# Attention on one core: the values' matmuls between a step's two score pairs, both maxima behind the second

## The chip, the cores and the metric

The kernel runs on one core of a Trainium2 chip. The metric is the device time of one execution in microseconds. An engine's work is named as in the profile: PE is TensorE (PEld its weight loads), DVE VectorE, ACT ScalarE, POOL GpSimd, SP SyncE.

## The reference

Four blocks act on x (4 batches of 512 tokens, 512 wide): a quantised gated linear layer, a mixture of experts, cross attention with rotary positions, and a second mixture of experts. The change lies in the attention:

```python
q = (x @ Wq).reshape(b, n, N_HEADS, HEAD_DIM)       # 32 heads of 16
k, v = jnp.split(ctx @ Wkv, 2, axis=-1)
q = apply_axial_rope(q, pos_map)
k = apply_axial_rope(k, ctx_pos_map)
logits = jnp.einsum('bqhd,bkhd->bhqk', q, k) * scale
w = jax.nn.softmax(logits, axis=-1)
attn = jnp.einsum('bhqk,bkhd->bqhd', w, v)
return attn.reshape(b, n, N_HEADS * HEAD_DIM) @ Wout + bout
```

## The kernel before

`attention` (L1657) works on units of eight heads of one batch: (b, c) with c from 0 to 3, sixteen units in all. Every engine runs the same list of turns (`turns`, L1791): four turns for a batch -1 that only prepare, four for batch 0, a hardware loop over batches 1 and 2 (`Fori`), four for batch 3, and two that finish. A turn (b, c) has eight steps. In each step of TensorE's turn:

- `scores` (L1974) makes transposed scores of one head for 128 keys and 512 queries, in PSUM banks 4 and 5 in turn; four of them a step (h = 0 to 3), S0 to S3 below. Each waits until ScalarE's exponential of two scores before (`exp_done`) has left its bank. ScalarE's `exps` (L2083) writes E, E0 to E3 below.
- `maxima` (L1988) makes scores of a later unit the other way round, two heads at once for 128 queries, in banks 0 and 1 (pair 0) or 2 and 3 (pair 1). VectorE reduces each pair to row maxima (`a_top`, L2223), 16 reductions a turn, number n = 2 * step + pair. The next `maxima` into the same banks waits for that reduction (`maxed`). After reduction 7 `cut_max` (L2184 to L2192) splits the maxima into three bfloat16 parts; slot 10 turns them, ScalarE copies them, and GpSimd writes them to memory and back into the rows of Q (L1901, L1910), for the scores of the next unit.
- `values` (L2006) multiplies V by the exponentials of the step before, into bank 6: four heads in four column strips, float32. After the fourth and the eighth step ScalarE copies bank 6 (`take_sum`, L2092).
- `slot(n)` (L1959) runs the side jobs of `jobs(b, c, n)` (L1765). All use bank 7. Before a job TensorE waits until the one before it has been consumed (`DONE`, L1953). The kinds: "x" turns the normalised tokens (L1924, consumed by ScalarE), "q" projects queries (L1929, ScalarE), "o" turns the values' result (L1940, VectorE normalises it, L2202 and L2208), "a" turns the attention output (L1945, ScalarE), "m" turns the maxima (L1934, ScalarE), "p" is the output projection of 128 tokens (L1950; VectorE adds it into X, L2214).

Every turn has q in slot 0, o in slots 4 and 11, a in 8, m in 10. A turn with c == 0 has besides p in slots 12, 14 and 15 and x in 13 and 15 (behind p); one with c == 1 has two x ahead of q in slot 0 and p in slot 2. The c == 0 turn of batch 3 has no x.

VectorE's turn goes through n = 0 to 15: reduction n, then the tasks of n, then the consumption of a job of slot n:

```python
for fn in tasks[n]:
    fn()
outs(n)
```

The tasks of every turn are the pair swap of q behind reduction 2 (L2173) and `cut_max` behind 7. At c == 0 come the next batch's statistics behind 0 to 3, their aggregation behind 4 (ScalarE takes the root at the start of step 3, L2097, with two loads of its function table), the normalisation behind 8 (L2155) and the bias behind 12 (L2161).

Of the kernel before, what the change touches and what calls it, by code (L numbers as in the profile page):

```python
# [1425 lines left out]
class SideJobs:  # L1426
# [55 lines left out]
    def count(self, b, kind, n):  # L1482

        return b * len(self.JOBS) + self.JOBS.index((kind, n)) + 1
# [172 lines left out]
def attention(nc, X, PS, identf, identb, ones_b, tg, ln_eps, tgate, Wq, Wout, bout, tables_dram, k_parts, v_dram, routed):  # L1657
# [22 lines left out]
    with ExitStack() as s:  # L1680
# [69 lines left out]
        def is_unit(b, c):  # L1750
            return not isinstance(b, int) or 0 <= 4 * b + c < NU
# [4 lines left out]
        def before(b, c, n):  # L1756

            c -= n
            while c < 0:
                b, c = b - 1, c + DC  # L1760
            while c >= DC:
                b, c = b + 1, c - DC
            return b, c
# [40 lines left out]
        def n_unit(unit, per=1):  # L1804

            b, c = unit
            return b * (DC * per) + (c + 1) * per

        def n_ring(unit, per):

            return (unit[0] + 1) * per
# [9 lines left out]
        def n_st(unit, step, h):  # L1821
            b, c = unit
            return b * (DC * 32) + c * 32 + step * 4 + h + 1
# [12 lines left out]
        def is_first(unit, n=1):  # L1836

            return isinstance(unit[0], int) and 4 * unit[0] + unit[1] - n < 0
# [75 lines left out]
        @block.tensor  # L1914
        def _(pe):
            pe.wait_ge(w_loaded, 48)
            B = PS[:, 7, :]

            def do(kind, unit, extra):
                b, c = unit  # L1920
                if kind == "x":
                    pe.wait_ge(xh_ready, b + 1)
                    for t in range(TB):
                        last = nc.tensor.transpose(B[:, t * P:(t + 1) * P], xh[:, t, extra * P:(extra + 1) * P], identf[:])  # L1924
                    last.then_inc(x_turned, 1)
                if kind == "q":
                    pe.wait_ge(xT_ready, (b + 1) * DC)
                    for d in range(DC):
                        last = nc.tensor.matmul(B, wq[:, d, c * P:(c + 1) * P], xT[:, d, :], start=(d == 0), stop=(d == DC - 1))  # L1929
                    last.then_inc(q_turned, 1)  # L1930
                if kind == "m":
                    pe.wait_ge(mcut_ready, n_unit(unit))
                    for t in range(TB):
                        last = nc.tensor.transpose(PS[0:3 * HU, 7, t * 64:(t + 1) * 64].bitcast(BF16),  # L1934
                                                   mcut[:, t].rearrange("p i h -> p (i h)"), identb[:])
                    last.then_inc(m_turned, 1)
                if kind == "o":
                    pe.wait_ge(OT_ready, n_unit(unit, 2) - 1 + extra)
                    for t in range(TB):
                        last = nc.tensor.transpose(B[:, t * P:(t + 1) * P], OT[:, t * P:(t + 1) * P], identf[:])  # L1940
                    last.then_inc(o_turned, 1)
                if kind == "a":
                    pe.wait_ge(o_normed, n_unit(unit, 2))
                    for t in range(TB):
                        last = nc.tensor.transpose(B[:, t * P:(t + 1) * P], attn[:, t, c * P:(c + 1) * P], identf[:])  # L1945
                    last.then_inc(a_turned, 1)
                if kind == "p":
                    pe.wait_ge(aT_ready, (b + 1) * DC)
                    for d in range(DC):
                        last = nc.tensor.matmul(B, attnT[:, d, extra * P:(extra + 1) * P], wo[:, d, :], start=(d == 0), stop=(d == DC - 1))  # L1950
                    last.then_inc(projected, 1)

            DONE = {"x": (xT_ready, lambda u, e: u[0] * DC + e + 1), "q": (qf_ready, lambda u, e: n_unit(u)),  # L1953
                    "m": (mT_ready, lambda u, e: n_unit(u)), "o": (o_normed, lambda u, e: n_unit(u, 2) - 1 + e),
                    "a": (aT_ready, lambda u, e: n_unit(u)), "p": (x_added, lambda u, e: u[0] * TB + e + 1)}
            prior = [None]

            def turn(b, c):
                def slot(n):  # L1959
                    for job in jobs(b, c, n):  # L1960
                        if prior[0] is not None:

                            sem_, count = DONE[prior[0][0]]
                            pe.wait_ge(sem_, count(prior[0][1], prior[0][2]))
                        do(*job)
                        prior[0] = job

                if not isinstance(b, int) and c == 0:

                    prior[0] = [j for n in range(16) for j in jobs(*before(b, c, 1), n)][-1]  # L1970
                if isinstance(b, int) and b == NB - 1 and c == 0:
                    prior[0] = [j for n in range(16) for j in jobs(b - 1, DC - 1, n)][-1]

                def scores(unit, step, h):  # L1974
                    if not is_unit(*unit):
                        return
                    k, head, kt = unit[1], (step // 4) * 4 + h, step % 4
                    if step == 0 and h == 0:
                        pe.wait_ge(m_loaded, n_unit(unit, 32))
                        if is_first(unit):  # L1980
                            pe.wait_ge(ones_ready, 4 * RING)
                    if not (is_first(unit) and step == 0 and h < 2):
                        pe.wait_ge(exp_done, n_st(unit, step, h) - 2)
                    o, rows_ = head % 2, (MAX_AT[0] + 3, P)[head % 2]
                    nc.tensor.matmul(PS[:, 4 + h % 2, :], K6[k][0:rows_, o, head // 2, kt * P:(kt + 1) * P], Q6[k][0:rows_, o, head // 2, :],  # L1985
                                     start=True, stop=True).then_inc(st_done, 1)

                def maxima(unit, h, pair):  # L1988
                    if not is_unit(*unit):
                        return  # L1990
                    k = unit[1]
                    if h == 0 and pair == 0:
                        pe.wait_ge(kv_loaded[k], n_ring(unit, 16 * (2 * SLOTS + 1)))
                        pe.wait_ge(q_loaded[k], n_ring(unit, 16 * 2 * SLOTS))
                        if is_first(unit):
                            pe.wait_ge(ones_ready, 4 * RING)
                    if not (is_first(unit) and h == 0):
                        pe.wait_ge(maxed, n_max(unit, h, pair) - 2)
                    t = 2 * (h % 2) + pair
                    for o in range(2):  # L2000
                        at = slice(o * FOUR, (o + 1) * FOUR)
                        last = nc.tensor.matmul(PS[:, 2 * pair + o, :], Q6[k][at, o, h // 2, t * P:(t + 1) * P], K6[k][at, o, h // 2, :],  # L2002
                                                start=True, stop=True)
                    last.then_inc(scored, 1)

                def values(unit, step):  # L2006
                    if not is_unit(*unit):
                        return
                    k, kt = unit[1], step % 4
                    pe.wait_ge(exp_done, n_st(unit, step, 3))  # L2010
                    if kt == 0 and not (is_first(unit) and step == 0):

                        pe.wait_ge(OT_ready, n_unit(unit, 2) - 2 + step // 4)
                    for h in range(4):
                        last = nc.tensor.matmul(PS[32 * h:32 * h + 32, 6, :], V[k][:, kt, (step // 4) * 4 + h, :], E[step % 2][:, h, :],  # L2015
                                                start=(kt == 0), stop=(kt == 3))
                    last.then_inc(pv_done, 1)

                heads = max_heads(b, c)
                for step in range(8):  # L2020
                    scores((b, c), step, 0)
                    scores((b, c), step, 1)
                    maxima(*heads[step], 0)
                    slot(2 * step)
                    scores((b, c), step, 2)
                    scores((b, c), step, 3)
                    maxima(*heads[step], 1)
                    if step == 0:
                        values(before(b, c, 1), 7)
                    else:  # L2030
                        values((b, c), step - 1)
                    slot(2 * step + 1)

            turns(pe, turn)
# [574 lines left out]
```

## Time and profile before

| | |
|---|---|
| median of 3 runs | 1495.58 us (1495.02 to 1496.68) |
| the profiled execution | 1494.6 us, its span 1493.1 us |
| TensorE busy | 1186.9 us |
| VectorE busy | 847.4 us |
| ScalarE busy | 649.5 us |
| GpSimd busy | 401.5 us |
| mean granted clock of TensorE | 0.902 of full speed |

The attention's first score starts at 794.29 us of the span and its last values' matmuls at 1322.48 us. A profile's time is that of one execution; the span runs from its first to its last instruction. Busy times of matmuls overlap with those of weight loads, and the ends of matmuls are modelled.

### The profile page before, as it was taken

What the parts mean: (1) busy time and instruction counts of PE and PEld (TensorE: products, weight loads), DVE (VectorE), ACT (ScalarE), POOL (GpSimd) and SP (SyncE); (2) the same over time, 40 slices, a digit from 0 to 9 for tenths busy, and PEclk for the clock granted to TensorE, in tenths of its full rate; (3) what the DMA queues carried; (4) which work ended last, traced back from release to release, by engine and by line L of the source; (5) the groups of instructions that cost most, each with busy time, mean ns of one, the idle gap of its engine ahead of it and who ended that gap; (6) DMA issues with size and microseconds to landing.
All of it is one profiled execution on the core that took longest, in us unless ns stands there. A gap on an engine that the chain in (4) does not pass through costs nothing. (4 is left out here: it accounts for less than half of the span.)

```text
span 1493.1 us, 18209 instructions
## 1 busy us (share of the span) xinstructions
PE 1186.9 (79%) x5251; PEld 517.3 (35%) x5317; DVE 847.4 (57%) x1314; ACT 649.5 (44%) x1145; POOL 401.5 (27%) x474
## 2 busy tenths in 40 slices
PE   2657566679988999993337899899899999875897
PEld 2333334345544444441101222332232223222453
DVE  3585857641344555521468787667757776415534
ACT  1333232345532222226304666556746665733543
POOL 0505051411113222212453332222303320005332
PEclk8777787889998999997657999999999999996999
DMA  5141311244324444426163332222312330007011
GB/s 197 43 140 34 126 69 57 95 162 136 113 96 170 157 143 147 139 92 200 57 186 104 98 108 75 78 69 81 92 47 84 94 90 7 3 1 85 29 43 43
DMA packets 106348, 141.46 MB, mean 95 GB/s; under 512 B 20788, under 2 KB 75572, under 8 KB 106280
## 3 DMA queue, kind: packets, MB, share of 16 engines
q1 hardware_dynamic: 87912, 111.77, 23.1%
q0 software_dynamic: 18368, 28.85, 7.4%
q8 instruction: 35, 0.57, 0.2%
q14 instruction: 33, 0.27, 0.1%
HBM read 97.44 MB, written 46.27 MB: 96 GB/s over the span
## 5 line engine op out<-in xcount | busy, mean ns | idle before, releaser
L2223 DVE TENSOR_REDUCE a_top<-PS 128x2 f32<-128x1024 f32 x256 | 309.3, 1223 | 114.7 <-PE PS L2002 107.6
L2083 ACT ACTIVATE a_E<-PS 128x512 f32<-128x512 f32 x512 | 277.7, 597 | 134.7 <-PE PS L1985 134.6
L1985 PE MATMUL PS<-a_Q,a_K 99*128 99x512 bf16 (+1 forms) x467 | 161.3, 391 | 33.2 <-ACT a_E L2083 20.5
L1251 PE MATMUL PS<-f_W,f_GT 128*128 x312 | 142.2, 599 | 0.0
L2002 PE MATMUL PS<-a_K,a_Q 64*128 64x512 bf16 x512 | 105.0, 408 | 43.6 <-issue 19.3
L2015 PE MATMUL PS<-a_E,a_V 128*32 128x512 f32 x1024 | 138.0, 612 | 0.4 <-ACT a_E L2083 0.4
L1985 PEld LDWEIGHTS PS<-a_Q,a_K 99*128 99x128 bf16 (+1 forms) x512 | 41.5, 97 | 188.7 <-ACT a_E L2083 165.7
L1307 DVE TENSOR_TENSOR f_H<-f_SG,PS 128x256 f32<-128x256 f32 x39 | 16.4, 422 | 125.8 <-ACT f_SG L1291 125.8
L1251 PEld LDWEIGHTS PS<-f_W,f_GT 128*128 128x128 f32 x312 | 57.2, 193 | 57.5 <-issue 57.5
L1641 POOL TENSOR_TENSOR a_qf<-a_qf,a_tab 128x512 f32<-128x512 f32 x16 | 20.6, 1290 | 206.6 <-DVE a_swapped L2173 206.6
L1270 PE MATMUL PS<-f_W,f_HT 128*128 x156 | 73.3, 593 | 0.0
L2002 PEld LDWEIGHTS PS<-a_K,a_Q 64*128 64x128 bf16 x512 | 24.7, 94 | 130.0 <-issue 79.8
L1929 PE MATMUL PS<-a_xT,a_wq 128*128 128x512 f32 x128 | 64.4, 650 | 3.7 <-ACT a_xT L2056 3.0
L1291 ACT ACTIVATE f_SG<-PS 128x256 f32<-128x256 f32 x39 | 14.9, 383 | 110.7 <-PE PS L1251 110.7
L2544 PE MATMUL PS<-f_W,f_xb 128*128 128x512 bf16 x249 | 61.9, 391 | 0.5 <-issue 0.2
L1950 PE MATMUL PS<-a_wo,a_attnT 128*128 128x512 f32 x128 | 59.2, 605 | 3.7 <-DVE X L2214 2.6
L837 PE MATMUL PS<-f_W,f0r_xT 128*128 128x512 f32 x128 | 58.3, 598 | 0.0
L1351 POOL DMA_INDIRECT a_rows<-f_y,l_pos x32 | 36.3, 1135 | 68.3 <-POOLq L54 40.6
L2334 POOL TENSOR_TENSOR f_H<-f_HF,f_gates 128x512 bf16<-128x512 f32 x32 | 33.4, 1044 | 73.5 <-DVE f_HF L2415 73.5
L1297 ACT COPY f_Y<-PS 128x512 f32<-128x512 f32 x39 | 22.8, 585 | 60.5 <-PE PS L1270 60.5
L1217 POOL DMA_INDIRECT f_G<-f_xn,f_idx x39 | 41.0, 1050 | 29.4 <-POOL f_idx L1214 28.7
L2415 DVE TENSOR_TENSOR f_HF<-f_SG,PS 128x512 f32<-128x512 f32 x32 | 22.0, 688 | 46.5 <-ACT f_SG L2473 46.5
(351 smaller groups left out, 1982.1 us busy)
## 6 DMA issues: line engine op xcount, KB each, us to landing
f0r_raw<-in_L_ffn_W_dram SPq DMA_DIRECT2D x24, 512.0 KB, 5.3
a_K<-k_parts SPq DMA_DIRECT2D x192, 64.0 KB, 2.2
a_Q<-a_q_parts SPq DMA_DIRECT2D x192, 64.0 KB, 2.2
f_y<-f_Y SPq DMA_DIRECT2D x39, 256.0 KB, 2.0
v_units<-V SPq DMA_DIRECT2D x16, 512.0 KB, 3.7
a_V<-v_units SPq DMA_DIRECT2D x16, 512.0 KB, 3.5
k_parts<-f_k_parts SPq DMA_DIRECT2D x16, 384.0 KB, 3.4
a_q_parts<-a_parts SPq DMA_DIRECT2D x16, 384.0 KB, 2.6
```

The lines of the kernel that those rows point to most:

```text
L837: last = nc.tensor.matmul(PS[:, 5, 0:2 * I], xT[b % 2][:, c, t * P:(t + 1) * P], W13[:, E, c, :], start=(c == 0), stop=(c == DC - 1))
L1217: pool.indirect_dma_start(out=G[k][:], out_offset=None, in_=xn_dram, in_offset=bass.IndirectOffsetOnAxis(ap=idx[:, k:k + 1].bitcast(U32), ...
L1251: last = nc.tensor.matmul(PS[:, 2 + k % 2, 0:2 * I], GT[k][:, c, :], W13[:, bass.ds(e, 1), c, :].rearrange("p a n -> p (a n)"), start=(c = ...
L1270: last = nc.tensor.matmul(PS[:, 6 + k % 2, :], HT[k][:, c, :], W2[:, bass.ds(e, 1), c, :].rearrange("p a n -> p (a n)"), start=(c == 0), s ...
L1929: last = nc.tensor.matmul(B, wq[:, d, c * P:(c + 1) * P], xT[:, d, :], start=(d == 0), stop=(d == DC - 1))
L1950: last = nc.tensor.matmul(B, attnT[:, d, extra * P:(extra + 1) * P], wo[:, d, :], start=(d == 0), stop=(d == DC - 1))
L1985: nc.tensor.matmul(PS[:, 4 + h % 2, :], K6[k][0:rows_, o, head // 2, kt * P:(kt + 1) * P], Q6[k][0:rows_, o, head // 2, :], start=True, st ...
L2002: last = nc.tensor.matmul(PS[:, 2 * pair + o, :], Q6[k][at, o, h // 2, t * P:(t + 1) * P], K6[k][at, o, h // 2, :], start=True, stop=True)
L2015: last = nc.tensor.matmul(PS[32 * h:32 * h + 32, 6, :], V[k][:, kt, (step // 4) * 4 + h, :], E[step % 2][:, h, :], start=(kt == 0), stop=( ...
L2083: nc.scalar.activation(E[step % 2][:, h, :], PS[:, 4 + h % 2, :], ACT.Exp).then_inc(exp_done, 1)
L2223: nc.vector.tensor_reduce(top[:, h - h % 2:h - h % 2 + 2, t], PS[:, 2 * pair:2 * pair + 2, :], AX.X, ALU.max).then_inc(maxed, 1)
L2544: last = nc.tensor.matmul(PS[:, 2 * h + m, :], xb[b % 2][:, c, t * P:(t + 1) * P], W13[:, c, m, h * HE:(h + 1) * HE, :].rearrange("p e i - ...
```

## The change

In each step the values move from behind the second maxima to between the score pairs, behind the even slot; the first maxima move to behind the second score pair, so that both stand there together. The odd slot stays last. ScalarE's, VectorE's, GpSimd's and SyncE's programs are as before.

```diff
                 for step in range(8):
                     scores((b, c), step, 0)
                     scores((b, c), step, 1)
-                    maxima(*heads[step], 0)
                     slot(2 * step)
-                    scores((b, c), step, 2)
-                    scores((b, c), step, 3)
-                    maxima(*heads[step], 1)
                     if step == 0:
                         values(before(b, c, 1), 7)
                     else:
                         values((b, c), step - 1)
+                    scores((b, c), step, 2)
+                    scores((b, c), step, 3)
+                    maxima(*heads[step], 0)
+                    maxima(*heads[step], 1)
                     slot(2 * step + 1)
```

TensorE in turn (3, 0), before: from the values of step 5 through the projection of slot 12 to that of slot 14. L1985 are scores, L2002 maxima (two matmuls a pair), L2015 values, L1940 the transposes of slot 11, L1950 projections.

```order
L2015 MATMUL PS<-a_E,a_V 32x512 x4
L1940 MATMUL PS<-identf,a_OT 128x128 x4
L1985 MATMUL PS<-a_Q_0,a_K_0 128x512 x2
L2002 MATMUL PS<-a_K_2,a_Q_2 128x512 x2
L1950 MATMUL PS<-a_wo,a_attnT 128x512 x4
L1985 MATMUL PS<-a_Q_0,a_K_0 128x512 x2
L2002 MATMUL PS<-a_K_2,a_Q_2 128x512 x2
L2015 MATMUL PS<-a_E,a_V 32x512 x4
L1985 MATMUL PS<-a_Q_0,a_K_0 128x512 x2
L2002 MATMUL PS<-a_K_2,a_Q_2 128x512 x2
L1950 MATMUL PS<-a_wo,a_attnT 128x512 x4
```

The same place after the change:

```order
L2015 MATMUL PS<-a_E,a_V 32x512 x4
L1985 MATMUL PS<-a_Q_0,a_K_0 128x512 x2
L2002 MATMUL PS<-a_K_2,a_Q_2 128x512 x4
L1940 MATMUL PS<-identf,a_OT 128x128 x4
L1985 MATMUL PS<-a_Q_0,a_K_0 128x512 x2
L1950 MATMUL PS<-a_wo,a_attnT 128x512 x4
L2015 MATMUL PS<-a_E,a_V 32x512 x4
L1985 MATMUL PS<-a_Q_0,a_K_0 128x512 x2
L2002 MATMUL PS<-a_K_2,a_Q_2 128x512 x4
L1985 MATMUL PS<-a_Q_0,a_K_0 128x512 x2
L1950 MATMUL PS<-a_wo,a_attnT 128x512 x4
```

Both maxima of a step are now one row of four matmuls behind its second score pair, and no maxima stand between the first score pair and a projection. The values follow the projection directly.

TensorE in the loop's turn (b, 0), before: from the projection of slot 12 to the transposes of slot 13 (L1924).

```order
L1950 MATMUL PS<-a_wo,a_attnT 128x512 x4
L1983 REGISTER_ALU
L1985 MATMUL PS<-a_Q_0,a_K_0 128x512
L1983 REGISTER_ALU
L1985 MATMUL PS<-a_Q_0,a_K_0 128x512
L1998 REGISTER_ALU
L2002 MATMUL PS<-a_K_2,a_Q_2 128x512 x2
L2015 MATMUL PS<-a_E,a_V 32x512 x4
L1964 REGISTER_ALU
L1922 REGISTER_ALU
L1924 MATMUL PS<-identf,a_xh 128x128 x4
```

After the change, from directly behind that projection:

```order
L2015 MATMUL PS<-a_E,a_V 32x512 x4
L1983 REGISTER_ALU
L1985 MATMUL PS<-a_Q_0,a_K_0 128x512
L1983 REGISTER_ALU
L1985 MATMUL PS<-a_Q_0,a_K_0 128x512
L1998 REGISTER_ALU
L2002 MATMUL PS<-a_K_2,a_Q_2 128x512 x2
L1998 REGISTER_ALU
L2002 MATMUL PS<-a_K_2,a_Q_2 128x512 x2
L1964 REGISTER_ALU
L1922 REGISTER_ALU
L1924 MATMUL PS<-identf,a_xh 128x128 x4
```

The maxima whose reductions VectorE makes ahead of the bias and of the add of this projection stood ahead of the projection; now only the values, two scores and the maxima themselves stand between the projection and the transposes.

## Rows read from the trace of the kernel before

**Rows 1.** The page, section 1: busy us, share of the span, instructions

```profile
PE 1186.9 (79%) x5251; PEld 517.3 (35%) x5317; DVE 847.4 (57%) x1314; ACT 649.5 (44%) x1145; POOL 401.5 (27%) x474
```

**Rows 2.** Busy time by window, one turn each: (1,0), (1,3), (2,1), (3,0)

```profile
core 0: us, PE busy (x) PEld busy (x) DVE busy (x) ACT busy (x) POOL busy (x), PEclk, DMA share, GB/s
...
928.57:976.81 48.24, 42.10 (x191) 14.38 (x192) 30.11 (x43) 24.62 (x46) 8.99 (x10) 0.96 0.22 65
1039.80:1069.91 30.11, 27.82 (x151) 8.14 (x153) 23.19 (x28) 19.51 (x38) 8.99 (x10) 1.00 0.28 85
...
1117.77:1150.64 32.87, 31.25 (x159) 9.58 (x160) 23.04 (x28) 19.59 (x38) 8.99 (x10) 1.00 0.26 77
...
1210.86:1247.12 36.26, 34.70 (x168) 11.11 (x169) 24.91 (x30) 19.68 (x38) 8.99 (x10) 1.00 0.24 71
```

**Rows 3.** Timeline of a plain step: start us, us, engine, line, operation, count, idle before

```profile
1127.30 1.06 PE L2015 MATMUL PS<-a_E,a_V 128*32 128x512 f32 x8
...
1128.30 0.61 PE L1985 MATMUL PS<-a_Q,a_K 99*128 99x512 bf16 x2
...
1128.80 2.16 ACT L2083 ACTIVATE a_E<-PS 128x512 f32<-128x512 f32 x4 [0.93 <-PE PS L1985]
...
1128.84 0.39 PE L2002 MATMUL PS<-a_K,a_Q 64*128 64x512 bf16 x2
...
1129.45 0.88 PE L1985 MATMUL PS<-a_Q,a_K 99*128 99x512 bf16 x2 [0.23 <-ACT a_E L2083]
...
1129.94 0.10 PEld L1985 LDWEIGHTS PS<-a_Q,a_K 128*128 128x128 bf16 x1 [0.39 <-ACT a_E L2083]
...
1130.58 1.06 PE L2015 MATMUL PS<-a_E,a_V 128*32 128x512 f32 x8
```

**Rows 4.** Groups of VectorE, attention, 794 to 1346 us: busy us, mean ns | idle before

```profile
L2223 DVE TENSOR_REDUCE a_top<-PS 128x2 f32<-128x1024 f32 x233 | 282.7, 1223 | 101.9 <-PE PS L2002 94.9
L2208 DVE TENSOR_TENSOR a_attn<-PS,a_rsum 128x256 f32<-128x256 f32 x32 | 13.6, 424 | 1.3
L2214 DVE SCALAR_TENSOR_TENSOR X<-PS,tg,X 128x512 f32 (+1 forms) x16 | 12.0, 751 | 43.8 <-PE PS L1950 43.8
L2173 DVE STREAM_SHUFFLE a_swapped<-a_qf 128x512 f32<-128x512 f32 x13 | 9.5, 730 | 0.0
...
L2161 DVE TENSOR_TENSOR X<-X,a_tbias 128x2048 f32 (+1 forms) x3 | 6.8, 2281 | 0.0
...
L2155 DVE TENSOR_SCALAR a_xh<-X,a_mv,a_rstd 128x512 f32 (+1 forms) x12 | 5.7, 542 | 0.1
```

**Rows 5.** Timeline of the same turn, step 2: the job of slot 4

```profile
1125.87 0.66 PE L1940 MATMUL PS<-identf,a_OT 128*128 128x128 f32 x4
...
1126.36 0.68 PE L1985 MATMUL PS<-a_Q,a_K 99*128 99x512 bf16 x2
```

**Rows 6.** Timeline of turn (1,0), step 6: slot 12 and what VectorE does

```profile
951.45 3.70 PE L1950 MATMUL PS<-a_wo,a_attnT 128*128 128x512 f32 x8 [0.15 <-DVE a_attn L2208]
951.52 1.23 DVE L2223 TENSOR_REDUCE a_top<-PS 128x2 f32<-128x1024 f32 x1
...
952.66 2.28 DVE L2161 TENSOR_TENSOR X<-X,a_tbias 128x2048 f32 x1
954.99 0.60 PE L1985 MATMUL PS<-a_Q,a_K 99*128 99x512 bf16 x2
955.30 0.75 DVE L2214 SCALAR_TENSOR_TENSOR X<-PS,tg,X 128x512 f32 x1 [0.36 <-PE PS L1950]
```

**Rows 7.** Timeline of turn (2,1): first and last of the five passes of cut_max

```profile
1131.95 0.19 DVE L2184 TENSOR_SCALAR a_ntop<-a_top 128x32 f32<-128x32 f32 x1
...
1132.83 0.19 DVE L2192 TENSOR_TENSOR a_mcut<-a_ntop,a_mcut 128x32 bf16<-128x32 f32 x1
```

**Rows 8.** Timeline of turn (1,0), step 3: scores behind the table loads, then values

```profile
939.48 0.88 PE L1985 MATMUL PS<-a_Q,a_K 99*128 99x512 bf16 x2 [2.21 <-ACT a_E L2083]
...
940.64 1.94 PE L2015 MATMUL PS<-a_E,a_V 128*32 128x512 f32 x8
```

**Rows 9.** Busy time by window, one us of the same place, columns as in rows 2

```profile
941.00:942.00 1.00, 1.00 (x8) 0.00 (x0) 0.97 (x1) 0.00 (x0) 0.18 (x1) 0.50 0.00 0
```

## The prediction

> **What bounds the kernel now.** I read the page first: TensorE is busy for 79% of the span, VectorE for 57%, ScalarE for 44% [rows 1]. The change touches attention alone, so I cut that part into its turns (one turn is one unit of eight heads of one batch, eight steps) and looked at one window each [rows 2]. An ordinary turn takes 30.11 us. A turn with c == 0, at a batch boundary, takes 48.24 us, one with c == 1 32.87 us, and the c == 0 turn of the last batch, which has no next batch to prepare, 36.26 us. TensorE is busy for 42.1 of the 48.24 us, so there its waits already cost 6 us.
>
> Then I read a step with no side job in order of time [rows 3]. Below, S0 to S3 are the four score matmuls, M0 and M1 the two maxima, V the values, E0 to E3 the exponentials. V starts at 1127.30, S0 at 1128.30, E0 at 1128.80, and the four exponentials run without a gap for 2.16 us, 0.54 each. M0 starts at 1128.84. S3 has to wait for E1, which ends at 1129.88, and its weights load at 1129.94; the next V starts at 1130.58. So the step is a loop over two engines: V 1.00, S0 to E0 0.50, two exponentials 1.08, handoff 0.06, S3 and M1 0.64: 3.28 us. TensorE waits for ScalarE twice in it (0.23 and 0.39 us), and ScalarE then idles for 1.1 us while V and S0 run. VectorE needs two reductions of 1.22 us a step [rows 4] and is no bound here.
>
> **The change in a step without a job.** No instruction is added or removed. V moves up between S1 and S2, so it runs while E0 and E1 do, and the loop becomes S1 to V 0.32 (the spacing of S3, M1 and V in [rows 3], 0.64 for two), V to S2 1.00, S2 to E2 0.50, E2 and E3 1.08, handoff 0.1 to S1 of the next step: 3.0 us. With V at 0 the step reads: S2 1.00, S3 1.22, M0 1.54, M1 1.86, S0 2.18 (E2 ends at 2.04), S1 2.64 (E3 ends at 2.58), V 2.96 to 3.01. So TensorE has some 0.2 us of room. Gain 0.27 us a plain step.
>
> **Steps with a job.** A small job in an even slot was free before: the four transposes at 1125.87 delay S2 only to 1126.36, within the wait for E0 [rows 5]. Now it lies between S1 and V, on the loop: +0.49. A job in an odd slot was fully on the path (0.49) and is now partly inside the wait for E3: it starts at 2.18, S0 follows at 2.67, S1 at 2.89 instead of 2.64, so it costs 0.25. A projection or a q job takes 3.54 us on the path in both orders (951.45 to 954.99 in [rows 6]). The copy of the values by ScalarE delayed E0 by 0.2 us once or twice a turn; that falls away. An ordinary turn is then three steps of 3.01, two of 3.50, 3.4 with slot 10, 3.25 with slot 11 and 6.55 with q: 29.2 us against 30.11. Against that stands VectorE: M0 and M1 now come together late in the step, with 0.4 us of room before M1 must wait for the reduction of the step before. The normaliser of slots 4 and 11 (0.42 and a reciprocal before it), the swap (0.73) and the cutting of the maxima (five small passes, 1131.95 to 1133.02) use that up [rows 4, 7]. Following the reductions through the turn at 1.22 each, the second one of step 2 ends 0.5 us after M1 of step 3 could start; that M1 waits, and the V behind it comes 0.2 us late. So **-0.7 us a turn**. There are four such turns in the loop (-2.8); the three of batch 0, where VectorE also adds expert rows, give -1.0 together and the three last turns of batch 3 -0.7. Sum **-4.5**.
>
> **Where VectorE hands back.** All side jobs use one bank, and each waits until the one before has been consumed. VectorE consumes a projection only after its reduction with the same slot number. Before, M0 stood ahead of the even slot, so that reduction ran under the 3.54 us projection [rows 6]: reduction at 951.52, bias at 952.66 to 954.94, and the add into X at 955.30, 0.31 us after TensorE had left the projection. Now M0 comes only after the projection, V, S2 and S3. Set V to 0: M0 starts at 1.54, its reduction at 1.97 and ends at 3.20, the add (0.75) at 3.95, handoff 4.05.
>
> - c == 1, slot 2: the projection's add also stands behind the swap, so slot 4's transpose starts at 4.85, where its place would be 2.96: **+1.9**, three turns: **+5.7**.
> - c == 0 in the two loop batches, slot 12: the next batch's normalisation (four passes of 0.54 in a row) stands behind reduction 8. With V of step 4 at 0: reduction 8 ends at 3.2, the normalisation at 5.4, reduction 9 at 6.65, and M1 of step 5, which could start at 5.2, waits for it until 6.75. Reductions 10 and 11 end at 7.9 and 9.1, the normaliser at 9.85, and the projection starts at 9.95, 2 us after S1; V of step 6 comes at 13.5 instead of 10.5 now. The cutting and the slower steps ahead add 0.4, and a fall of the clock there 1.0: **+4.4**.
> - Slot 13: the transpose waits for reduction 12, the bias (2.28) and the add: 6.4 us after V instead of 1.0. What TensorE can do meanwhile (scores, maxima) ends at 2.2. V to V becomes 11.3 instead of 6.73: **+4.6**.
> - Slot 15: the projection waits for reduction 14 and its add, 4.05 instead of 1.0; without the 0.85 us tail behind q this is 16.6 instead of 14.25: **+2.4**.
> - The wait of 4.2 us in slot 13 comes ahead of a projection. After a shorter wait, 2.21 us, the trace shows V taking 1.94 instead of 1.06 us [rows 8], at a granted clock of 0.50, the 1.2 GHz level [rows 9]. The turn's mean clock is 0.96 [rows 2], so some 3.9 of its 48.24 us ran at half speed. One fall costs from 0.9 (what V lost) to 1.9 us (half of 3.9). The projection behind the wait is all TensorE, so I take the upper end: **+2.0**.
> - That is 13.4 a turn, two turns: **+26.8**. The steps before slot 11 break even: they are paced by the statistics and the root's table loads in both orders.
> - c == 0 of batch 3 has no bias and no transposes: slots 12, 14 and 15 wait 2.0, 1.35 and 1.4 us, less 0.5 for its other steps: **+4.2**. The first attention turn has no projections; the maxima behind its reductions and slot 15's transpose give **+2.1**.
>
> The warm-up turns hold maxima alone, with VectorE busy behind them: nothing from the change, with -1 to +2 as bounds. SyncE's loads are for units three turns ahead: nothing. GpSimd's write and reload of the maxima starts 0.5 us later after its transpose and has 0.3 us of room left by my count; if it misses, up to 1 us in some turns.
>
> Sum: -4.5 + 5.7 + 26.8 + 4.2 + 2.1 = **+34.3 us**. The profiled execution took 1494.6 us (span 1493.1), which gives 1528.9; the median of the runs is 1.0 higher: **1530 us**.
>
> On the clock the Trainium skill (TensorE: Matmul & The Clock Gate, Why this matters for your kernels) tells one to avoid idle gaps between bursts of matmuls. [rows 8, 9] agree. [...]
>
> **The rivals.**
> 1. *The steps win* (faster). If VectorE's adds were ready in time, because it runs ahead of TensorE in these turns, only the loop of 3.0 us would count: 0.9 us in each of some 12 turns, -11, 1485 us; the place is slot 13, and it decides once reduction, bias and add together take less than the 0.6 us between M0 and that slot. For it: a plain step does hold 0.6 us of TensorE waits [rows 3]. Against it: the three take 1.22, 2.28 and 0.75 us [rows 4], and none can start before M0 is done. The Trainium skill (Perfetto Trace Analysis, Optimization Strategy) says to find the gaps of the most contended engine and let what they wait for start sooner. That is this rival: by it the 79% busy TensorE would decide the time.
> 2. *A wash*: the c == 1 waits and half the boundary waits are absorbed by ScalarE slack; within 3 us of 1495.6.
> 3. *Half of it*: VectorE catches up where I count it late, and the clock holds: c == 0 turns cost 6 to 8 us each, 1512 to 1518.
> 4. *More*: the clock stays at half through the boundary chain (the projection and the q job, 3.54 us each, double), or M1 stalls in every step: a further 12 to 20 us, 1542 to 1550.
>
> **How the numbers follow.** My forecast 0.58, rival 3 0.18, rival 4 0.14, rival 1 0.06, rival 2 0.04. The range leaves out rivals 1 and 2, half of rival 4 and little else: 1511 to 1546. A measurement of this kernel can tell about 0.2%, 3 us. Slower by more: 0.9. Within: 0.04. Faster: 0.06.
>
> **What would show it.** The gap between V rows in a plain step of an ordinary turn falls from 3.28 to 3.0 us, and the ordinary turn to 29.4 us. In a c == 0 turn TensorE's transposes for xT wait about 4 us for VectorE's add into X, the turn takes about 61 us, and the granted clock falls behind it. The c == 1 turn shows slot 4's transpose waiting 1.9 us. VectorE's reductions come in pairs. If the boundary turns stay near 48 us, or ordinary steps stay at 3.28, the argument is wrong.

## The result, and the profile after

| | before | changed |
|---|---|---|
| median of the runs | 1495.3 us (4 runs) | 1528.82 us (4 runs, 1527.09 to 1532.44) |
| ratio to before, 95% interval | | 1.0228 [1.0206, 1.0251] |
| the profiled execution | 1494.6 us, span 1493.1 | 1532.44 us, span 1530.8 |
| TensorE busy | 1186.9 us | 1204.1 us |
| VectorE busy | 847.4 us | 842.3 us |
| mean granted clock | 0.902 | 0.891 |

The changed kernel is 33.5 us slower by the medians; 34.3 were forecast as the sum of the terms. Its profiled execution is the slowest of its four, 3.6 us above their median, so the rows below add up to more: their spans differ by 37.7 us.

The page of the changed kernel, section 1, answers [rows 1]:

```profile
PE 1204.1 (79%) x5316; PEld 520.9 (34%) x5317; DVE 842.3 (55%) x1314; ACT 649.9 (42%) x1145; POOL 399.2 (26%) x474
```

No engine has more work to do. Of TensorE's 17 us more of busy time 12 lie in the two boundary turns of the loop, where the granted clock is lower (5.7 in (1,0), 6.5 in (2,0)); 5.5 lie outside of the attention, where no instruction was changed and the trace before has some records fewer. Busy time by window, the changed kernel, one turn each in this order: (0,1), (1,0), (1,1), (1,2), (3,0). It answers [rows 2]; the last three columns are the granted clock, the DMA share and GB/s.

```profile
842.54:871.89 29.35, 27.39 (x153) 7.98 (x152) 23.81 (x29) 19.62 (x37) 11.12 (x12) 1.00 0.34 105
930.62:993.67 63.05, 47.80 (x193) 16.17 (x192) 30.39 (x44) 24.76 (x44) 8.98 (x10) 0.86 0.16 49
993.67:1027.95 34.28, 32.13 (x162) 9.17 (x161) 22.33 (x28) 19.62 (x37) 9.00 (x10) 0.95 0.25 75
1027.95:1056.91 28.96, 27.40 (x154) 7.87 (x153) 22.47 (x27) 19.63 (x37) 8.99 (x10) 1.00 0.28 89
1241.09:1281.53 40.44, 34.79 (x169) 10.68 (x168) 24.14 (x30) 18.64 (x36) 9.00 (x10) 1.00 0.21 63
```

A turn is counted from its first values row to that of the next turn. The ordinary turn has fallen from 30.11 to 28.96 us. The boundary turn (1,0) has risen from 48.24 to 63.05, with its clock down from 0.96 to 0.86; (2,0) went from 47.86 to 63.57. c == 1 is at 34.28 and 33.33 against 32.88 and 32.87, (3,0) at 40.44 against 36.26. The gain sits in the turns that have no projection.

The timeline of turn (1,3), changed kernel, from the values at 1059.95 to the next step's scores, answers [rows 3]:

```profile
1059.95 1.07 PE L2015 MATMUL PS<-a_E,a_V 128*32 128x512 f32 x8
...
1060.95 0.61 PE L1985 MATMUL PS<-a_Q,a_K 99*128 99x512 bf16 x2
1061.37 2.24 ACT L2083 ACTIVATE a_E<-PS 128x512 f32<-128x512 f32 x4 [0.49 <-PE PS L1985]
...
1061.49 0.61 PE L2002 MATMUL PS<-a_K,a_Q 64*128 64x512 bf16 x4
...
1062.03 0.88 PE L1985 MATMUL PS<-a_Q,a_K 99*128 99x512 bf16 x2
1062.51 0.10 PEld L1985 LDWEIGHTS PS<-a_Q,a_K 128*128 128x128 bf16 x1 [0.39 <-ACT a_E L2083]
```

S2 follows the values by 1.00 us, E2 follows S2 by 0.42, and S1 of the next step loads its weights at 1062.51, just behind E3. Behind this S1 come the transposes of slot 4, so the first plain distance from values to values is the next one, 2.88 us. Around it ScalarE pauses for 0.49 to 0.65 us between its exponentials, and for 1.08 behind the transposes, where a plain step had 0.93 to 1.12.

The timeline of the boundary turn (1,0), changed kernel, from the values of step 6 at 960.66 to slot 13 and 14, answers [rows 6]:

```profile
960.66 1.07 PE L2015 MATMUL PS<-a_E,a_V 128*32 128x512 f32 x8
961.66 0.61 PE L1985 MATMUL PS<-a_Q,a_K 99*128 99x512 bf16 x2
...
962.20 0.60 PE L2002 MATMUL PS<-a_K,a_Q 64*128 64x512 bf16 x4
962.63 1.23 DVE L2223 TENSOR_REDUCE a_top<-PS 128x2 f32<-128x1024 f32 x1 [5.66 <-PE PS L2002]
963.77 2.28 DVE L2161 TENSOR_TENSOR X<-X,a_tbias 128x2048 f32 x1
966.29 0.75 DVE L2214 SCALAR_TENSOR_TENSOR X<-PS,tg,X 128x512 f32 x1 [0.23 <-DVE X L2161]
966.96 1.21 DVE L2223 TENSOR_REDUCE a_top<-PS 128x2 f32<-128x1024 f32 x1
967.17 1.11 PE L1924 MATMUL PS<-identf,a_xh 128*128 128x128 f32 x4 [4.37 <-DVE X L2214]
...
968.96 5.00 PE L1950 MATMUL PS<-a_wo,a_attnT 128*128 128x512 f32 x8
973.88 1.07 PE L2015 MATMUL PS<-a_E,a_V 128*32 128x512 f32 x8
```

This is the chain of the prediction, link by link. VectorE had been idle for 5.66 us, under the projection; then the maxima come at 962.20, and reduction, bias and add run one behind the other. TensorE sits idle for 4.37 us (4.2 forecast). The next projection takes 5.00 instead of 3.70 us, at a granted clock of 0.50, as the windows show (columns as above):

```profile
964.00:966.00 2.00, 0.00 (x0) 0.00 (x0) 2.00 (x1) 0.00 (x0) 0.00 (x0) 0.69 0.00 0
966.00:968.00 2.00, 0.83 (x4) 0.84 (x5) 1.76 (x3) 0.00 (x0) 0.00 (x0) 0.50 0.00 0
968.00:970.00 2.00, 2.00 (x6) 0.69 (x5) 0.17 (x1) 1.59 (x3) 0.00 (x0) 0.50 0.00 0
```

The waits of TensorE in the attention, changed kernel (us in total, times, longest):

```profile
PE PS L2002 <- DVE a_top L2223: 17.4, 32, 2.2
PE PS L1985 <- ACT a_E L2083: 11.5, 13, 2.3
PE PS L1924 <- DVE X L2214: 10.6, 4, 4.4
PE PS L1950 <- DVE X L2214: 8.9, 7, 1.8
PE PS L1950 <- DVE a_attn L2208: 4.4, 3, 1.5
PE PS L1940 <- DVE X L2214: 4.1, 3, 1.6
```

In the kernel before, the same six lines read 1.6, 20.5, 1.9, 2.6, 0.2 and nothing. So TensorE waits 9.0 us less for ScalarE's exponentials. In exchange it waits 28.0 us for VectorE at side jobs (the last four lines) instead of 4.7, and its maxima wait 17.4 us for reductions instead of 1.6.

### The profile page after: what moved, and what is told of

Its sections match the earlier page's. It is cut to its first block and busy times, and to the rows that moved or that the text cites. A ratio compares the mean times of both kernels' runs of the same rounds, so it can differ in the third digit from the quotient of the medians.

```text
span 1530.8 us, 18274 instructions
## 1 busy us (share of the span) xinstructions
PE 1204.1 (79%) x5316; PEld 520.9 (34%) x5317; DVE 842.3 (55%) x1314; ACT 649.9 (42%) x1145; POOL 399.2 (26%) x474
## 5 line engine op out<-in xcount | busy, mean ns | idle before, releaser
L2223 DVE TENSOR_REDUCE a_top<-PS 128x2 f32<-128x1024 f32 x256 | 302.6, 1219 | 175.0 <-PE PS L2002 172.5
L1985 PE MATMUL PS<-a_Q,a_K 99*128 99x512 bf16 (+1 forms) x512 | 172.9, 395 | 20.1 <-ACT a_E L2083 11.5
L2015 PE MATMUL PS<-a_E,a_V 128*32 128x512 f32 x1024 | 138.9, 612 | 2.7 <-ACT a_OT L2092 1.2
L2002 PE MATMUL PS<-a_K,a_Q 64*128 64x512 bf16 x512 | 90.4, 403 | 51.5 <-DVE a_top L2223 33.0
L1985 PEld LDWEIGHTS PS<-a_Q,a_K 99*128 99x128 bf16 (+1 forms) x512 | 38.8, 97 | 195.4 <-ACT a_E L2083 164.7
L1950 PE MATMUL PS<-a_wo,a_attnT 128*128 128x512 f32 x128 | 68.5, 685 | 14.1 <-DVE X L2214 8.9
L2002 PEld LDWEIGHTS PS<-a_K,a_Q 64*128 64x128 bf16 x512 | 19.1, 94 | 122.6 <-DVE a_top L2223 61.7
L1924 PE MATMUL PS<-identf,a_xh 128*128 128x128 f32 x64 | 14.1, 360 | 54.0 <-DVE a_xh L2155 38.5
```

The lines of the kernel that those rows point to most:

```text
L2223: nc.vector.tensor_reduce(top[:, h - h % 2:h - h % 2 + 2, t], PS[:, 2 * pair:2 * pair + 2, :], AX.X, ALU.max).then_inc(maxed, 1)
```

## The experiments

All times stand beside runs of the kernel before on the same chip, whose median was 1495.7 us in the first four experiments, 1493.94 in the next four and 1494.5 in the last.

**One half at a time.** First the values alone are moved, with the first maxima left ahead of the even slot.

```diff
                     scores((b, c), step, 1)
+                    maxima(*heads[step], 0)
                     slot(2 * step)
...
                     scores((b, c), step, 3)
-                    maxima(*heads[step], 0)
                     maxima(*heads[step], 1)
```

> Edit: the values stand between the score pairs as in the changed kernel, but the first maxima stay ahead of the even slot, as before. Theory (the loss is VectorE's late consumption of the projections, because the first maxima stand behind them; the gain is the shorter loop of a plain step): the boundary turns (c == 0) go back to about 48 us and c == 1 to 33 us; the plain step becomes 2.88 + 0.32 = 3.2 us, because the first maxima now stand on the loop between S1 and the values, and small jobs in even slots stay on the loop, so an ordinary turn is 30 to 30.6 us. Total 1492 to 1499 us. Rival (moving the values is what costs, because it puts them behind the projections and in front of the score pair whose exponentials ScalarE needs): boundary turns stay above 58 us and the total near 1525 us.

Measured: 1510.34 us, ratio 1.0100 [1.0083, 1.0117]. The windows of turns (1,0), (1,1) and (1,2):

```profile
930.03:979.05 49.02, 41.35 (x190) 14.10 (x193) 30.18 (x43) 24.63 (x44) 8.98 (x10) 1.00 0.21 63
979.05:1013.33 34.28, 32.10 (x159) 9.53 (x161) 23.12 (x28) 19.73 (x37) 9.00 (x10) 1.00 0.26 75
1013.33:1043.97 30.64, 28.46 (x150) 8.07 (x152) 22.36 (x27) 19.74 (x37) 8.99 (x10) 1.00 0.28 84
```

The boundary turn is back at 49.0 us and the plain step reads 3.21, both as the theory said; so the loss there is not the values' place alone. The total was outside my range. The even slot's jobs pass from free to paid in every turn, a projection or q step takes 6.84 instead of 6.25 us, and I had put c == 1 at 33 where it is 34.28. The fifteen turns from (0,1) on take 0.4 to 2.2 us more each, the first 1.8 less, 14 in all. The mechanism held, my total for it did not.

Then the maxima alone: both behind the second score pair, the values behind them, as before.

```diff
                     scores((b, c), step, 1)
                     slot(2 * step)
-                    values(...)
                     scores((b, c), step, 2)
                     scores((b, c), step, 3)
                     maxima(*heads[step], 0)
                     maxima(*heads[step], 1)
+                    values(...)
                     slot(2 * step + 1)
```

> Edit: both maxima behind the second score pair as in the changed kernel, but the values behind them, as before. Theory: the plain step's loop keeps its old form with one more pair of maxima in it, 3.28 + 0.32 = 3.6 us, and the projections still wait for VectorE, with the values' 1.0 us as additional cover: boundary turns 58 to 62 us. Total 1540 to 1560 us, slower than the changed kernel. Rival (the position of the values is the cause of the loss): total near 1495 to 1510 us.

Measured: 1533.79 us, ratio 1.0257 [1.0236, 1.0277]. The same three turns:

```profile
936.91:993.61 56.70, 43.41 (x192) 15.16 (x193) 30.59 (x45) 24.52 (x45) 8.98 (x10) 0.94 0.18 55
993.61:1027.69 34.08, 30.14 (x160) 9.39 (x161) 22.34 (x29) 19.53 (x38) 9.02 (x10) 1.00 0.26 76
1027.69:1059.01 31.32, 27.15 (x153) 7.89 (x153) 22.08 (x28) 19.51 (x38) 8.98 (x10) 1.00 0.28 82
```

The rival falls: without moving the values the kernel loses as much, and against the changed kernel the intervals overlap. The plain step is 3.50 us (3.6 forecast), the boundary turn 56.7 (58 to 62 forecast), and the total lies below my 1540 to 1560: three misses on the same side. So the late maxima cost in both kinds of turn; the values' move earns 0.6 us a plain step against this order. In turn (1,0) the two halves do not add up: the values alone cost 0.8 us, the maxima alone 8.5, both together 14.8. With both moved the maxima start later behind a projection, because the values stand ahead of them, and the mean clock is 0.86 instead of 0.94; how the remaining 5.5 us divide between these two was not measured.

**Where in the program the loss is.** The new order in the c == 0 turns alone, and in the c == 2 and 3 turns alone, with the old order elsewhere:

```diff
+                new = c == 0
...
+                    if not new:
+                        maxima(*heads[step], 0)
                     slot(2 * step)
...
```

> Edit: the new order only in the turns with c == 0, the old order everywhere else. Theory: the loop's boundary turns take 62 to 64 us each instead of 48, turn (3,0) 40.4 instead of 36.3, the first 2 to 4 us more; total 34 to 39 us above the kernel before, 1530 to 1534 us, the whole loss of the changed kernel in four of its twenty turns. Rival (the loss is spread over the turns): total below 1515 us.

Measured: 1531.29 us, ratio 1.0259 [1.0234, 1.0283]. Its turn (1,0) and (1,1):

```profile
926.30:989.51 63.21, 47.84 (x196) 16.13 (x199) 31.62 (x45) 25.19 (x46) 8.98 (x10) 0.89 0.16 49
989.51:1022.39 32.88, 31.25 (x159) 9.58 (x160) 23.02 (x28) 19.59 (x38) 8.99 (x10) 1.00 0.25 79
```

This order loses 37 us with only the turns with c == 0 changed, so the changed kernel's whole loss is there. The c == 1 turn is as before.

The other one has `new = c >= 2`, for the four batches:

> Edit: the new order only in the turns with c == 2 and c == 3 of the four batches, the old order everywhere else. Theory (the gain lies in the ordinary turns, the loss in the turns with projections): these eight turns take what they take in the changed kernel, 0.2 us less in batch 0, 0.9 to 1.2 us less in the loop, 0.2 in turn (3,2), and the boundary turns stay at 48 us. Total 3.5 to 6 us below the kernel before: 1490 to 1492 us. Rival (the shorter steps bring work forward that then waits at the next boundary turn): 1494 to 1496 us.

Measured: 1491.56 us, ratio 0.9983 [0.9970, 0.9996] over 12 runs. Its turn (1,2) takes 28.99 us, as in the changed kernel, and the boundary turn (2,0) 48.24. The turns beside them can't be read alone, because the values, by which turns are counted, change their place at a border between the orders: (1,1) reads 31.60 and (1,3) 30.45. The three together take 91.03 us instead of 93.10, so this batch gains 2.1 us, as much as (1,2) and (1,3) of the changed kernel did; batch 2 gains 1.8, batches 0 and 3 nothing to speak of. The total lies in the range. The distance to before is 2.4 us by the medians, less than the 3.5 to 6 I gave, and its interval, 0.6 to 4.5, reaches into them.

**The links of the chain.** The bias addition moved behind reduction 13, so that the projection's add comes first:

```diff
-                    at(12, add_bias)
+                    at(13, add_bias)
```

> Edit: the changed kernel, with VectorE's bias addition (2.28 us) as the task behind reduction 13 instead of 12, so that the add of slot 12's projection comes first. Theory: the wait of slot 13's transposes falls from 4.37 to 2.1 us in each of the three batches' boundary turns that have it and the two loop turns lose the 2.28 us and part of the clock fall: 2.3 to 4.5 us each, total 5 to 11 us below the changed kernel. Rival (the bias is hidden behind another wait): no change.

Measured: 1521.75 us, ratio 1.0159 [1.0129, 1.0189]: 7 us below the changed kernel by the medians, in the range. The timeline of its turn (1,0):

```profile
952.39 6.56 PE L1950 MATMUL PS<-a_wo,a_attnT 128*128 128x512 f32 x8 [1.69 <-DVE a_attn L2208]
...
961.99 0.74 DVE L2214 SCALAR_TENSOR_TENSOR X<-PS,tg,X 128x512 f32 x1
...
962.86 0.65 PE L1924 MATMUL PS<-identf,a_xh 128*128 128x128 f32 x4 [1.84 <-DVE X L2214]
...
963.77 2.28 DVE L2161 TENSOR_TENSOR X<-X,a_tbias 128x2048 f32 x1
```

The wait of slot 13 is 1.84 us instead of 4.37. The turn still takes 61.6 us: the projection of slot 12 takes 6.56 us here instead of 3.70, behind a wait of only 1.69.

Next, the first maxima are put back ahead of the even slots that hold a projection. There are nine such steps, three in each of batches 1 to 3 (the expectation counts seven):

```diff
+                    early = any(kind == "p" for kind, unit, extra in jobs(b, c, 2 * step))
+                    if early:
+                        maxima(*heads[step], 0)
                     slot(2 * step)
...
+                    if not early:
+                        maxima(*heads[step], 0)
                     maxima(*heads[step], 1)
```

> Edit: the changed kernel, but in the seven steps whose even slot holds a projection (slots 12 and 14 at c == 0, slot 2 at c == 1) the first maxima stand ahead of the slot, as before. Theory: the waits for VectorE behind these projections go, the boundary turns fall from 63 to 46 to 49 us, c == 1 from 33.3 and 34.3 to 32 to 32.5, the ordinary turns stay at 29.0. Total 1483 to 1491 us, below the kernel before. Rival (the clock or VectorE's backlog from pairs of reductions holds the boundary turns up): boundary turns stay above 56 us, total above 1508.

Measured: 1500.73 us, ratio 1.0028 [1.0014, 1.0043] over 7 runs. That takes back 28 of the 33.5 us, with the ordinary turn at 28.96, but it misses the range: the boundary turns take 52.57 and 50.69 us, not 46 to 49. Slot 12 shows why:

```profile
954.34 3.48 DVE L2227 TENSOR_REDUCE a_top<-PS 128x2 f32<-128x1024 f32 x3
955.61 0.39 PE L2002 MATMUL PS<-a_K,a_Q 64*128 64x512 bf16 x2 [1.42 <-DVE a_top L2227]
...
958.49 3.70 PE L1950 MATMUL PS<-a_wo,a_attnT 128*128 128x512 f32 x8 [1.15 <-DVE a_attn L2212]
958.56 1.23 DVE L2227 TENSOR_REDUCE a_top<-PS 128x2 f32<-128x1024 f32 x1
959.70 2.28 DVE L2165 TENSOR_TENSOR X<-X,a_tbias 128x2048 f32 x1
962.12 1.06 PE L2015 MATMUL PS<-a_E,a_V 128*32 128x512 f32 x8
962.35 0.75 DVE L2218 SCALAR_TENSOR_TENSOR X<-PS,tg,X 128x512 f32 x1 [0.36 <-PE PS L1950]
```

Reduction, bias and add are under the projection again. What stays is the lateness of the steps ahead: the maxima of steps 4 and 5 are still behind the scores, so reduction 9, the last of step 4, starts only behind the normalisation, the second maxima of step 5 wait 1.42 us for it, and the projection waits 1.15 us for slot 11's normaliser.

**A better order.** If the maxima must be early for VectorE and off the path for TensorE, they can be issued one step ahead, in TensorE's wait for ScalarE at a step's end:

```diff
                 heads = max_heads(b, c)
+                maxima(*heads[0], 0)
                 for step in range(8):
...
-                    maxima(*heads[step], 0)
                     maxima(*heads[step], 1)
+                    if step < 7:
+                        maxima(*heads[step + 1], 0)
                     slot(2 * step + 1)
```

> Edit: the values between the score pairs as in the changed kernel, but the first maxima of each step from 1 to 7 are issued at the end of the step before, behind its second maxima and ahead of its odd slot; those of step 0 at the start of the turn. Theory: the plain step keeps 2.88 us, because these maxima lie in TensorE's wait for ScalarE, and VectorE's reduction and adds run under the projections again, so ordinary turns stay at 29, c == 1 falls to 32.3 to 33.3, the loop's boundary turns to 46 to 50 us. Total 1480 to 1490 us, faster than both kernels. Rival (the pairing of reductions keeps VectorE late in the boundary turns): 50 to 53 us each as in the run with the maxima moved back at the projections alone, total 1495 to 1501.

Measured: 1489.02 us, ratio 0.9962 [0.9949, 0.9976] over 6 runs. Its turns (1,0), (1,1), (1,2):

```profile
923.67:972.52 48.85, 40.14 (x190) 13.80 (x193) 30.13 (x43) 24.75 (x44) 9.00 (x10) 1.00 0.20 63
972.52:1004.41 31.89, 29.96 (x158) 9.27 (x161) 22.35 (x28) 19.75 (x37) 9.01 (x10) 1.00 0.26 81
1004.41:1033.23 28.82, 26.87 (x152) 7.84 (x153) 22.03 (x27) 19.75 (x37) 9.01 (x10) 1.00 0.29 89
```

It has the short steps, 28.82 us in the ordinary turn and 31.89 at c == 1, and its side jobs wait 6.6 us for VectorE instead of the changed kernel's 28.0 (4.7 before). Its maxima do wait for reductions, 22.4 us in all, no more than 1.2 at a time. The boundary turns take 48.85 and 50.56 us against 48.24 and 47.86 before; the second lies above the 46 to 50 of the theory and in the range of the rival, whose total of 1495 to 1501 does not come. It is the fastest so far, 0.4% below the kernel before, and the interval is clear of 1.

With those maxima behind the odd slot instead of ahead of it:

> Edit: as the run with the next step's first maxima brought forward, but behind the odd slot instead of ahead of it. Theory: the same steps, but slot 13's and slot 15's jobs wait for VectorE before these maxima are issued, so reduction 14 and the add of slot 14 come later: slot 15's projection waits as long as it takes for reduction 14 behind slot 13's transposes, under slot 14's projection, so nothing. Total within 3 us of that run. Rival (VectorE's lateness in slot 11 decides): this one is better by 1 to 3 us, because slot 11's transposes no longer stand behind maxima that wait for reduction 10.

Measured: 1489.70 us, ratio 0.9963 [0.9947, 0.9979] over 7 runs. The two are equal, and the rival's 1 to 3 us do not show.

Last, the same with the old order at c == 0:

> Edit: the order of the run with the next step's first maxima brought forward, in all turns but those with c == 0, which keep the order of the kernel before. Theory (what that run still loses against the kernel before lies in its boundary turns, 48.9 and 50.6 instead of 48.2 and 47.9 us, where TensorE's waits bring the clock down): ordinary turns 28.8 to 29.2 us, c == 1 31.7 to 32.9, boundary turns 47.5 to 48.3; total 2 to 4 us below that run, 1485 to 1488 us. Rival (the boundary turns' loss is only a shift of their border with the next turn, since the values' place changes there): total equal to that run within 1.5 us, or above it.

Measured: 1491.08 us, ratio 0.9972 [0.9959, 0.9985] over 12 runs. The 1485 to 1488 do not come and the rival holds: the boundary turns read 48.55 and 48.67 us, but the turns ahead of them 30.39 and 30.10 instead of 29.19 and 28.90. Each pair takes 78.94 and 78.77 us together, against 78.04 and 79.46 in the run before the last, so the time is moved across the border between the two orders and not saved.

## Why the prediction was right

**The plain step.** Forecast 3.28 to 3.0 us, gain 0.27. Measured 2.88, gain 0.40. The loop was the right one. Most of the difference is "S2 to E2 0.50", taken from S0 to E0 before, which is 0.42 now.

**Steps with a job.** Forecast +0.49 for a small job in an even slot: slot 4's step takes 3.32 us against 2.88, so 0.44. In the old order it was 3.28, so such a job cancels the gain of its step, as forecast. The q step reads 6.32 (6.55 forecast), slot 11's 3.62 (3.25 forecast).

**The ordinary turn.** Forecast 29.4, measured 28.95 to 29.24, so the four in the loop give 4.2 us where 2.8 was forecast. Batch 0's three give 0.6 where 1.0 was forecast. The last three turns, for which a gain of 0.7 was forecast, take 1.8 us more: (3,1) and (3,2) gain 0.1 and 0.2, and (3,3) rises from 21.95 to 24.12. It holds no maxima, and a step without them read 2.88 us before the change already, as it does now; there was nothing to gain, while small jobs in even slots now cost 0.44, and the values of the last step come 2.56 us behind the ones before them instead of 0.88.

**c == 1.** The waits are there: slot 4's transposes wait for the add into X, 4.1 us in three turns (5.7 forecast). The turns themselves lost 1.4 and 0.5 us and (3,1) gained 0.1, 1.7 in all where the 5.7 stood beside turns that I had put at no change. So this term was too large by 4 us: 1.6 in the waits, the rest mostly because I gave (1,1) and (2,1) no gain of their other steps.

**The boundary turns.** Forecast +13.4 each, measured +14.8 and +15.7. Within (1,0): up to the values behind slot 12's projection +2.8 where +4.4 was forecast (1.0 of it for a fall of the clock that did not come there, and a wait of 1.46 instead of 2 us); from the values of step 6 to those of step 7 13.22 us where 11.3 and 2.0 for the clock were forecast; from there to the next turn 19.79 where 16.6 was forecast. The waits were right to some 0.5 us and the last link was wrong by 3.2, all clock: the projection of slot 15 takes 5.40 us and the q job 5.39, instead of 3.70 each. In (2,0), where these two take 3.70 and 3.69, the same stretch is 16.40.

**The clock.** This term was mis-sized: "+2.0" a turn, and 1.0 within the +4.4. The windows of (1,0) show the granted clock at 0.50 from 944, 965, 978 and 989 us of the span on, the first as in step 3 of the kernel before; (1 - 0.86) * 2 * 63.05 = 18 us ran at half speed, where the same sum gives 3.9 before. Windows in which it falls (columns as above):

```profile
944.00:946.00 2.00, 1.90 (x7) 0.34 (x8) 0.40 (x1) 1.54 (x3) 1.76 (x3) 0.57 0.00 0
...
978.00:980.00 2.00, 2.00 (x4) 0.73 (x4) 0.87 (x1) 0.00 (x0) 0.00 (x0) 0.61 0.00 0
...
988.00:990.00 2.00, 1.65 (x3) 0.70 (x4) 0.00 (x0) 0.22 (x1) 0.00 (x0) 0.67 0.00 0
```

The turn's three stretched side jobs alone cost 1.30 + 1.70 + 1.69 = 4.7 us, and the two of (2,0), 6.52 and 5.97 instead of 3.70, 5.1 us. An estimate from these rows: without the stretched jobs the two turns lose 10.1 and 10.6 us, where the terms without the clock's 3.0 were 10.4. So the waits were forecast well, and what the boundary turns lost above 13.4 is the clock. A fall follows some of the shorter waits and not others: slot 15's projection stands behind a wait of 1.76 us in both turns, and takes 5.40 us in (1,0) and 3.70 in (2,0).

**Batch 3 and the first turn.** (3,0): forecast +4.2, measured +4.18, at a granted clock of 1.00, so these are waits alone. The first turn: forecast +2.1, measured +3.2 from the attention's first score, which comes 0.5 us earlier. Behind the attention the trace is 1.4 us longer, which no term held.

**The sum.** By these traces the terms are -2.9 for the turns without a projection, +1.7 for the three with c == 1, +30.5 for the two boundary turns, +4.2 and +3.2, where -4.5, +5.7, +26.8, +4.2 and +2.1 were forecast. Terms that were wrong by 1 to 4 us on either side cancel, and the profiled execution is itself 3.6 us above the median. So the mechanism was right, and that the total came within 1 us of the 34.3 is in part luck.

**The rivals.** The steps did win what rival 1 said, near 1 us a turn, in the loop's four ordinary turns, and it decided nothing, since reduction, bias and add together take 4.3 us where rival 1 needed less than 0.6. Of rival 4, a clock at half through the boundary chain, a part occurred: in (2,0) slot 12's projection took 6.52 us, while slot 15's and the q job ran at full speed. Rival 3 needs boundary turns of 54 to 56 us and rival 2 shorter ones still; they take 63. The experiments carry the attribution: with the new order at c == 0 alone, the whole loss is there; with the first maxima ahead of the projections, 28 us of it go; with the bias behind the add, 7 go.

One thing stays open: how much of a boundary turn's loss would be left at a steady clock. The 10.1 and 10.6 us above are an estimate; I made no run that keeps TensorE busy through the waits, since the kernel uses all eight banks.

## What to carry to other kernels

An order is not judged by its commonest step. When an engine runs a fixed list, moving one producer behind a long job moves the consumer's whole queue, here a reduction, a bias and an add, from under that job to behind it; look up what stands in the consumer's list between that producer and the next thing that hands a buffer back. If a shorter loop and early producers both matter, issue the producers one step ahead, in the wait that the loop has anyway: that gave 0.4% where moving them back lost 2.3%. Both figures are of this kernel alone.

## What the runs showed of the hardware

The same short wait does not always cost the same. In turn (1,0) of the changed kernel slot 12's projection comes after a wait of 1.46 us and takes 3.70 us. In turn (2,0) it comes after 1.47 us and takes 6.52, at a granted clock of 0.50 (the 1.2 GHz level):

```profile
957.03 3.70 PE L1950 MATMUL PS<-a_wo,a_attnT 128*128 128x512 f32 x8 [1.46 <-DVE a_attn L2208]
...
1112.66 6.52 PE L1950 MATMUL PS<-a_wo,a_attnT 128*128 128x512 f32 x8 [1.47 <-DVE a_attn L2208]
```

```profile
1112.00:1114.00 2.00, 1.34 (x2) 0.82 (x3) 0.57 (x2) 0.18 (x1) 0.77 (x2) 0.50 0.71 250
```

The two waits are alike, and the projection behind them differs by 2.8 us; what decided it I did not find out. Nor does a fall wait for work to resume: in turn (1,0) TensorE is idle from 962.8 to 967.17, and the window from 964 to 966 shows no busy time and a granted clock of 0.69 already. Four runs of the kernel with the bias moved spread from 1514.4 to 1525.7 us, those with the values alone moved from 1509.9 to 1511.4; no run shows whether the falls make this difference.
